# Attention on one core: the product with v moved ahead of the third score product in each step

## The reference, cut to what matters

```
scores = einsum('bhtd,bhsd->bhts', q, k) / sqrt(hd)
attn = softmax(scores, axis=-1)
out = einsum('bhts,bhsd->bhtd', attn, v)
```

## Time and profile before

| | before |
|---|---|
| median of 3 runs | 4291.71 us (4291.42 to 4296.32) |
| profiled execution, first to last instruction | 4296.5 us |
| TensorE busy | 3510.7 us, 82% |
| VectorE busy | 2485.8 us, 58% |
| ScalarE busy | 2102.7 us, 49% |
| attention | about 124 to 1772 us of the span |

### The profile page before, as it was taken

One profiled execution on the slowest core, in us unless ns is written; L12 is line 12 of the kernel. 1 busy time (PEld: TensorE's weight loads), 2 busy tenths in 40 slices (PEclk: granted clock), 3 DMA queues, 4 the chain that ended last, 5 costly groups with the idle time before them and its releaser, 6 DMA issues. The chain is left out here.

```text
span 4296.5 us, 115371 instructions
## 1 busy us (share of the span) xinstructions
PE 3510.7 (82%) x41173; PEld 1852.0 (43%) x41175; DVE 2485.8 (58%) x5229; ACT 2102.7 (49%) x4024; POOL 1149.9 (27%) x2368
## 2 busy tenths in 40 slices
PE   8699999999999999732396977550869699898999
PEld 5232222322323222332264644440757566544678
DVE  7788888888888888580021238457245433235433
ACT  2488888888888888421143434320610022264322
POOL 1222222222222221124505844510533123210000
PEclk9799999999999999866698988555965599898999
DMA  1000000000000002534346533344723300233353
GB/s 53 7 6 6 6 6 7 6 6 6 6 7 6 6 6 89 189 102 139 136 137 195 161 118 124 122 140 150 246 84 75 86 15 0 84 135 125 108 188 125
DMA packets 288679, 345.07 MB, mean 80 GB/s; under 512 B 36768, under 2 KB 201632, under 8 KB 288544
## 3 DMA queue, kind: packets, MB, share of 16 engines
q1 hardware_dynamic: 254736, 297.27, 21.7%
q0 software_dynamic: 13328, 37.77, 2.7%
q10 hardware_dynamic: 20480, 8.40, 0.7%
HBM read 198.11 MB, written 135.79 MB: 78 GB/s over the span
## 5 line engine op out<-in xcount | busy, mean ns | idle before, releaser
L945 DVE TENSOR_REDUCE att_maxes<-att_ps_m 128x1 f32<-128x512 f32 x2048 | 1308.5, 686 | 230.9 <-PE att_ps_m L789 225.2
L900 ACT ACTIVATE att_prob<-att_ps_s 128x512 f32<-128x512 f32 x2048 | 1105.6, 599 | 222.5 <-PE att_ps_s L799 209.9
L799 PE MATMUL att_ps_s<-att_q_t,att_k_t 99*128 99x512 bf16 x2048 | 687.2, 386 | 8.7 <-ACT att_prob L900 7.9
L810 PE MATMUL att_ps_o<-att_prob,att_v_h 128*32 128x512 f32 x4096 | 546.4, 605 | 0.7 <-ACT att_prob L900 0.7
L787 PE MATMUL att_ps_m<-att_k_t,att_q_t 48*128 48x512 bf16 x1024 | 398.8, 389 | 16.3 <-DVE att_maxes L945 11.5
L789 PE MATMUL att_ps_m<-z_sb 48*128 48x512 bf16 x1024 | 399.3, 390 | 0.0
L787 PEld LDWEIGHTS att_ps_m<-att_k_t,att_q_t 48*128 48x128 bf16 x1024 | 94.6, 92 | 610.3 <-DVE att_maxes L945 509.8
L1570 DVE TENSOR_TENSOR experts_h<-experts_gs,experts_ps_g 128x128 f32<-128x128 f32 x192 | 55.3, 288 | 497.4 <-ACT experts_gs L1551 423.5
L698 POOL CAST att_max_parts<-att_neg_max 128x4 bf16<-128x4 f32 x128 | 24.9, 194 | 1154.1 <-DVE att_neg_max L952 1154.1
L799 PEld LDWEIGHTS att_ps_s<-att_q_t,att_k_t 99*128 99x128 bf16 x2048 | 157.7, 96 | 281.0 <-ACT att_prob L900 134.4
L1523 PE MATMUL experts_ps_g<-w_gu,experts_x_t 128*128 x768 | 225.1, 417 | 54.8 <-issue 41.0
(11 more groups left out here) (357 smaller groups left out, 6472.0 us busy)
## 6 DMA issues: line engine op xcount, KB each, us to landing
xf_t<-logits_t SPq DMA_DIRECT2D x16, 2048.0 KB, 8.5
slots_x<-zeros SPq DMA_DIRECT2D x97, 256.0 KB, 3.3
experts_xs<-slots_x SPq DMA_DIRECT2D x48, 512.0 KB
slots_y<-experts_y SPq DMA_DIRECT2D x48, 512.0 KB
logits_t<-sstat_logit SPq DMA_DIRECT2D x64, 256.0 KB
proj<-comb_pr SPq DMA_DIRECT2D x8, 1600.0 KB
mix_pr<-proj SPq DMA_DIRECT2D x32, 400.0 KB
gram_qk_in<-proj SPq DMA_DIRECT2D x32, 256.0 KB
```

The source lines that it names most:

```text
L799: pe.matmul(ps_s[bank(p, i)][:, :], k_t[0:ROWS, p, tile * P:(tile + 1) * P], q_t[0:ROWS, p, chunk * W:(chunk + 1) * W], start=True, stop=T ...
L810: mm = pe.matmul(ps_o[i * VW:(i + 1) * VW, :], v_h[:, p, group * GK + i, :], prob[:, (j * GK + i) % (RING * GK), :], start=(group == 0), s ...
L900: nc.scalar.activation(prob[:, i % (RING * GK), :], ps_s[bank(p, i)][:, :], ACT.Exp, scale=SCALE).then_inc(expd.sem, 1)
L945: v.tensor_reduce(maxes[:, p, tile, c:c + 1], ps_m[bank(p, i)][:, :], X, ALU.max).then_inc(reduced.sem, 1)
```

## The change

In `step` of the tensor block, the third score product (q = 2) no longer stands between the first pair of first-pass products and the product with v; it stands behind the second pair, directly ahead of the fourth. ScalarE, VectorE, GpSimd and SP have the same instructions in the same order as before.

```diff
                 if left >= 0:
                     score(n, p, j, 1)
                 seek(0)
-                if left >= 0:
-                    score(n, p, j, 2)
                 if j:
                     if left >= 0:
                         against_v(n, p, j - 1)
...
                     against_v(n - 1, 1 - p, STEPS - 1)
                 seek(2)
                 if left >= 0:
+                    score(n, p, j, 2)
                     score(n, p, j, 3)
```

## The result

| | before | changed |
|---|---|---|
| median of 4 runs | 4292.62 us (4291.42 to 4296.32) | 4393.38 us (4392.12 to 4395.58) |
| profiled span | 4296.5 us | 4391.7 us |
| ratio | | 1.0233, 95% interval 1.0219 to 1.0248 |

A forecast was written before the change was run, and what follows sets the result against it. The attention loop was taken as bound by TensorE's own succession of starts. A chunk changes by 0.78 - 0.10 - 0.10 + 0.23 = +0.81 us, over 124 chunks +100, giving 4391 us; range 4338 to 4414.

The forecast's parts named there:

- The copy of the output: Step g = 0 into g = 1: ScalarE's copy queues behind score product 2's late exponential; 4.06 for 3.28 us, +0.78.
- The bank wait: Score product 1 starts no sooner than 1.08 us after score product 2; step into g = 0 3.04 for 2.81, +0.23.
- The changes of form: TensorE's step has four changes of form instead of five, each costing 0.10 us; pair to product with v taken as 0.32.
- The lower bound of 0.22: Pair to product with v at 0.22 instead of 0.32 us: 50 us less, 4341; chance 0.15.
- the rule alone, which gave 4229: Rival: in the attention loop only changes of form count, other engines keeping pace; 63 us less, 4229; chance 0.03.
- The clock: Rival: idle TensorE lowers its clock in the attention loop; a tenth of steps slowed adds about 110 us, 4500; chance 0.03.
- The passages from odd to even heads: At 15 passages score product 1 waits for score product 3's exponential, about as long as today; put at 0.
- The last head: Plain step already bound by the same 1.08 us; copy costs at most 4 x 0.78 = 3 us, left to the range.
- The second rival: At g = 0 the bank holds score product 1 but the copy gets through: chunk 12.33, -9 us, 4283; chance 0.04.

The follow-up runs named there:

- Run 2: Kernel before with score product 2 moved behind the product with v, still ahead of the second pair: 4289.76 against 4230.1 us, ratio 1.0141.
- run 5: Changed kernel with TensorE's order of the kernel before at g = 0 alone: 4235.33 us against 4229.65 for the kernel before, ratio 1.0015.
- run 1: Changed kernel with ScalarE's output copy at g = 0 moved ahead of score product 2's exponential: 4209.06 us against 4230.1 for the kernel before, ratio 0.995.
- Run 6: Changed kernel with every exponential over 256 of 512 columns, half left out: 4276.87 us against 4229.65 for the kernel before, ratio 1.0115.
- run 7: Kernel before with score product 2 directly behind score product 1 at g = 1, 2 and 3, g = 0 as before: 4190.63 against 4229.65 us, ratio 0.9906.
- run 3: Kernel before, TensorE's order kept, with ScalarE's output copy at g = 0 ahead of score product 2's exponential: 4231.91 against 4230.1 us, ratio 1.0004.
- run 4: Kernel before with score product 2 moved earlier, directly behind score product 1 and ahead of the first pair: 4216.67 against 4230.1 us, ratio 0.9966.

## Why the prediction was right

The prediction held, in sign, size and mechanism. By its steps:

- **The copy of the output**, the largest term, was +0.78 a chunk and came to +0.79 (4.07 against 3.28). Run 2 shows it with no bank wait beside it, run 5 removes it through TensorE's order, run 1 through ScalarE's.
- **The bank wait** was taken as 1.08 us from product to product and is 1.08 in the plain step (+0.23 as forecast). Run 6 shows that it follows the length of the exponential. It is not a loss at g = 2 and 3, where transposes stand in between.
- **The changes of form.** The one unknown price, a pair followed by the product with v, was taken as 0.32 and is 0.32; so steps without a bank or copy wait are 0.10 shorter. The lower bound of 0.22, on which the low end of the range stood, was not needed. The Trainium skill ("TensorEngine Tiling (Array Packing)", Key Properties) says that a change of tiling mode drains TensorE; the traces agree in that a score product or pair that is followed by another form takes 0.10 us more, and they show that the rule alone, which gave 4229, doesn't decide: what one change less saves in a step is worth less than the waits that the new order makes. What TensorE does in the 0.10 us no trace shows.
- **The clock** stayed at 1.00 over the loop with about 1.1 us of idle TensorE in each chunk (4.07 - 3.25 and 3.04 - 2.78), as much as the rival had assumed, so that rival fell.
- **The passages from odd to even heads** were put at 0. Between copies two heads take 106.14 us now (310.81 to 416.95), 0.54 over 8 x 13.20; before it was 99.94 (250.84 to 350.78), 0.74 over 8 x 12.40. 15 x 0.20 is 3 us given back.
- **The last head** was put at 0, with up to 3 us left to the range, and both the text ahead of the prediction and the prediction took it to have no first pass. It has one in its first ten steps: in the trace of before its last pair starts at 1739.20, and only the steps behind that are like the earlier trace rows. From the copy in its first step to the copy behind its end it takes 48.72 us (1809.87 to 1858.59) where it took 45.00 (1711.87 to 1756.87), +3.7. The copy's wait is not all of it: its steps into g = 2 have no transposes of a coming head, and that of its second chunk, for one, goes from 2.81 us (1727.16 to 1729.97) to 3.11 (1825.95 to 1829.06) instead of becoming 0.10 shorter. These 3.7 us and the 3 given back at the passages cancel; that the sum came within 2 us is in this part luck.
- **A wrong reading that did no harm:** score product 2 lay 1.32 us ahead of the second pair in the order of before (1011.30 to 1012.62 in the earlier trace rows), not 1.64. With 1.08 us to a free bank it was free all the same, and the sum doesn't use the figure.
- **The second rival** (the copy gets through) had its step priced at 3.18; run 1, which makes it true, has 3.05. The failing term is the 0.29 us from score product 0 to the transposes, read from a row in which they waited for the copy (with the 0.50 behind it 0.79 us, where run 1 has 0.67). The rival would have been a gain of 21 us, 26 in the attention, not 9.

What stays open: no run shortened the copy itself or gave the score products a fourth bank, since the kernel spreads its tiles over all its banks already and taking one from the first pass wasn't tried; the rest of the program differed by 6 to 7 us between profiled executions on one chip (2584.3 to 2590.1 in runs 1 to 4, 2578.4 to 2585.8 in runs 5 to 7), and was some 60 us longer in the two executions of the result, and its cause wasn't sought. That is why the gain of run 7 in the attention is best read from its trace: 1605.8 us against 1646.3 in run 3, 40 less.

## What to carry to other kernels

When an instruction is moved on one engine, go through the hand-written queue of every engine that waits for it and ask what stands behind that wait: here a 0.6 us copy that fed TensorE stood behind the exponential of the moved product, and three quarters of the forecast's gross loss came from it, on an engine that was 85% busy and not the bound. Count banks in products, not in steps: with three banks, a fourth product in a row starts 1.08 us behind the first here, and other work has to stand between them. And a spacing taken from a trace is a price only if the later instruction waited for nothing; two of my three small misses (runs 1 and 3) came from spacings that held a wait, and the third (run 4) from a releaser's name that I took for one.

## What the runs showed of the hardware

- The tiled array can go from two 48-row products side by side to four 32-column products in 0.32 us from start to start, the same as from the pair to a score product and from a score product to either. Against the 0.22 us between score products that is 0.10 us for a change of form. The change behind the product with v isn't priced so exactly: the next start is 1.00 us behind it, for a pair as for a score product (run 2), 0.14 more than the 0.86 us of four products at that spacing, an estimate. Removing a change in a step is worth its price only where no other wait takes its place (run 7 against the changed kernel).
- ScalarE starts the next operation 0.46 to 0.48 us after the start of a copy of 0.58 to 0.59 us when its data is there (1066.92 to 1067.38 in the changed kernel, run 3), much as with exponentials (0.49).
- An order that leaves TensorE idle for 0.82 us once in each chunk of 13.2 us ran at the full 2.4 GHz (granted clock 1.00) throughout the loop.
